# Layer 0's entry by chunks of four tokens, modulation work on GpSimd, k scaled by a power

## The reference

```python
mod = (_silu(L0_c) @ L0_wmod).reshape(L0_c.shape[0], 6, 1, -1)
sa, ca, ga, sb, cb, gb = (mod[:, 0], mod[:, 1], mod[:, 2], mod[:, 3], mod[:, 4], mod[:, 5])
ga = (2 * (ga >= 0) - 1) * jnp.maximum(jnp.abs(ga), 0.25)
gb = (2 * (gb >= 0) - 1) * jnp.maximum(jnp.abs(gb), 0.25)
h = _layernorm(x, axis=-1) * (1 + ca) + sa
x = x + ga * _L0_attn_ref(h, ...)
```

```python
q = jax.nn.silu(x @ Wq).reshape(b, n, h, hd)
k = jax.nn.silu(x @ Wk).reshape(b, n, h, hd)
k = k * jax.lax.rsqrt(jnp.sum(k * k, -1, keepdims=True) + 1e-12)
v = (x @ Wv).reshape(b, n, h, hd)
beta = 2.0 * jax.nn.sigmoid(x @ Wbet)
a = jax.nn.sigmoid(x @ Wf)
def step(S, inp):
    qt, kt, vt, at, bt = inp
    Sd = at[..., None, None] * S
    u = vt - jnp.einsum('bhk,bhkv->bhv', kt, Sd)
    Sn = Sd + bt[..., None, None] * kt[..., None] * u[:, :, None, :]
    o = jnp.einsum('bhk,bhkv->bhv', qt, Sn)
    return (Sn, o)
```

## Time and profile before

| | before |
|---|---|
| median of 3 runs | 2143.96 us (2143.17 to 2151.37) |
| time of the profiled execution | 2147.42 us |
| its span | 2145.6 us |
| mean granted TensorE clock | 0.908 |
| busy: PE, DVE, ACT, POOL | 1723.7, 1363.8, 1163.1, 267.3 us |
| first instruction of the scan (L370) | starts at 75.19 us |

### The profile page before, as it was taken

One profiled execution on the slowest core, in us unless ns is written; L12 is line 12 of the kernel. 1 busy time (PEld: TensorE's weight loads), 2 busy tenths in 40 slices (PEclk: granted clock), 3 DMA queues, 4 the chain that ended last, 5 costly groups with the idle time before them and its releaser, 6 DMA issues.

```text
span 2145.6 us, 27944 instructions
## 1 busy us (share of the span) xinstructions
PE 1723.7 (80%) x10324; PEld 786.0 (37%) x10324; DVE 1363.8 (64%) x2683; ACT 1163.1 (54%) x2116; POOL 267.3 (12%) x336
## 2 busy tenths in 40 slices
PE   3599237269999999999875994989899988489998
PEld 2599225012222222222223442444444444334443
DVE  3898775599999999999622335556656656322222
ACT  3465103028888888888862336556666655212222
POOL 1265003000000000000000002111111111111110
PEclk7899658559999999999996996999999999699999
DMA  1000000430000000000012420000000000122320
GB/s 40 1 1 1 0 0 8 93 47 2 2 2 2 2 2 2 2 2 2 17 26 41 84 63 1 4 12 16 15 15 15 15 0 1 30 43 47 59 51 29
DMA packets 76094, 42.58 MB, mean 20 GB/s; under 512 B 21920, under 2 KB 72224, under 8 KB 75840
## 3 DMA queue, kind: packets, MB, share of 16 engines
q1 hardware_dynamic: 74576, 37.90, 8.6%
q10 hardware_dynamic: 1392, 3.02, 0.7%
HBM read 37.55 MB, written 3.15 MB: 19 GB/s over the span
## 4 chain that ended last, share of the span: by engine, by line
PE 52%; DVE 30%; ACT 7%; DMA 4%; issue 4%; POOL 1%; SPq 0%; ACTq 0%; DVEq 0%; POOLq 0%
DVE MX L865 17%; PE PS L1347 6%; PE PS L920 5%; PE PS L1353 5%; PE PS L1779 4%; PE PS L1780 4%; PE PS L1789 4%; PE PS L942 3%; DMA SB<-scr_w 3%; PE PS L433 3%; PE PS L1298 3%; ACT tmpb L986 3%; PE PS L1317 2%; PE PS L1189 2%; DVE MS L534 2%
## 5 line engine op out<-in xcount | busy, mean ns | idle before, releaser
L986 ACT ACTIVATE tmpb<-PS 128x512 f32<-128x512 f32 x1024 | 554.0, 595 | 143.0 <-PE PS L942 126.5
L865 DVE TENSOR_REDUCE MX<-PS 128x2 f32<-128x1024 f32 x512 | 585.3, 1217 | 52.7 <-PE PS L847 48.9
L920 PE MATMUL PS<-tmpb,VS 128*32 128x256 f32 x4096 | 326.4, 393 | 14.0 <-ACT tmpb L986 6.6
L847 PE MATMUL PS<-KST,QST 56*128 56x512 bf16 x1024 | 206.6, 401 | 61.6 <-DMA KST<-scr_k 34.3
L942 PE MATMUL PS<-QST,KST 59*128 59x512 bf16 x1024 | 201.4, 390 | 21.2 <-ACT tmpb L986 17.0
L1814 DVE TENSOR_TENSOR HG<-HG,PS 128x512 f32<-128x512 f32 (+1 forms) x96 | 65.9, 686 | 199.3 <-PE PS L1780 199.3
L1804 ACT ACTIVATE HG<-PS 128x512 f32<-128x512 f32 (+1 forms) x96 | 57.2, 595 | 207.7 <-PE PS L1779 207.7
L920 PEld LDWEIGHTS PS<-tmpb,VS 128*32 128x32 f32 x4096 | 82.5, 108 | 179.0 <-issue 85.0
L942 PEld LDWEIGHTS PS<-QST,KST 59*128 59x128 bf16 x1024 | 49.2, 93 | 244.3 <-ACT tmpb L986 229.8
L1347 PE MATMUL PS<-X,WF 128*128 128x512 f32 x256 | 128.4, 636 | 4.2 <-ACT X L1492 4.2
L1508 ACT ACTIVATE HF<-PS,CL 128x512 f32<-128x512 f32 x128 | 87.9, 687 | 68.7 <-PE PS L1347 68.7
(11 more groups left out here) (293 smaller groups left out, 2491.5 us busy)
## 6 DMA issues: line engine op xcount, KB each, us to landing
SB<-scr_w SPq DMA_DIRECT2D x16, 1024.0 KB, 14.4
WF<-in_L_attn_Wf SPq DMA_DIRECT2D x16, 256.0 KB, 3.0
QST<-NMP SPq DMA_DIRECT2D x192, 1.0 KB
G<-in_L_ffn_w SPq DMA_DIRECT2D x16, 176.0 KB, 2.4
QST<-scr_q SPq DMA_DIRECT2D x14, 192.0 KB
W<-in_L_ffn_w SPq DMA_DIRECT2D x16, 128.0 KB, 2.1
scr_q<-tmpb SPq DMA_DIRECT2D x3, 512.0 KB, 2.7
KST<-scr_k ACTq DMA_DIRECT2D x14, 96.0 KB
```

Of the source, the lines that this page charges most:

```text
L847: pe.matmul(PS[:, b + x, :], QST[r, 2 * g + jj, CH * qc + P * t:CH * qc + P * t + P], KST[r, g, cs(kc)], start=True, stop=True).then_inc(s ...
L865: r = v.tensor_reduce(MX[:, :, m // (TPC * NC), m // NC % TPC, m % NC], PS[:, b:b + 2, :], AX.X, ALU.max)
L920: last = pe.matmul(PS[32 * j:32 * j + 32, 3, h], VS[:, kt, u // NC, :], PB[:, kt % 2, j, h], start=(kt == 0 and half == 0), stop=(kt == NT ...
L986: a.activation(PB[:, kt % 2, j, :], PS[:, at % 3, :], ACT.Exp, scale=HD ** -0.5).then_inc(s_exp, 1)
```

## The change

The layernorm of the first chunk now needs only two modulation columns. x arrives in four transfers with a semaphore each. The two columns sa and ca of layer 0 are multiplied first (L273) and copied by DVE between two chunks' statistics. Chunks 0 and 1 are normalised and transposed through two PSUM banks, and projecting, normalising and k's products alternate by chunk. Of the other modulation vectors only what later code reads is computed: four rows of layer 0 in one matmul of 512 columns, and eight columns. Adding 1, the gates and Wo's two factors are done on POOL (`g_mods`). The Silu is a Sigmoid and a product. Instead of a square root on ACT and a reciprocal on DVE, POOL raises the sums of squares to -0.5, chunk by chunk, 128x64 numbers each (`g_krs`, L350). k's unit form of the last chunk is made in the second step of the scan. `s_mod` is waited for after the scan.

```diff
         def sp_pre(sp):
-            sp.dma_start(X[:, :, :], A["L0_attn_x"][0].rearrange("(p s) d -> p s d", p=P)).then_inc(s_x, 16)
+            for c in range(NC):
+                sp.dma_start(X[:, ts_(c), :], A["L0_attn_x"][0].rearrange("(p s) d -> p s d", p=P)[:, ts_(c), :]).then_inc(s_xc[c], 16)
...
         def act_pre(a):
             for l in range(2):
-                a.dma_start(ccol[:, l:l + 1], A[f"L{l}_c"].rearrange("a d -> d a")).then_inc(s_mod_in, 16)
-                a.dma_start(wm[:, l, :], A[f"L{l}_wmod"]).then_inc(s_mod_in, 16)
-            a.wait_ge(s_mod_in, 64)
-            a.activation(scol[:, :], ccol[:, :], ACT.Silu).then_inc(s_sc, 1)
+                a.dma_start(ccol[:, l:l + 1], A[f"L{l}_c"].rearrange("a d -> d a")).then_inc(s_cc, 16)
+            for l in range(2):
+                a.dma_start(wm[:, l, :], A[f"L{l}_wmod"]).then_inc(s_wm[l], 16)
+            a.wait_ge(s_cc, 32)
+            a.activation(sgc[:, :], ccol[:, :], ACT.Sigmoid).then_inc(s_sg, 1)
...
+        def pe_mods(pe):
+            pe.wait_ge(s_wm[1], 16)
+            pe.wait_ge(s_mc, 1)
+            pe.matmul(ROW, scb[:, :], wm[:, 0, 2 * D:6 * D], start=True, stop=True)
+            for l, j in ((0, 3), (0, 4), (1, 0), (1, 1), (1, 2), (1, 3), (1, 4), (1, 5)):
+                last = pe_col(pe, l, j)
             last.then_inc(s_modps, 1)
...
+        def pe_a0(pe):
+            pe_first_cols(pe)
+            pe.wait_ge(s_const, 1)
+            pe_turn_x(pe, 0)
+            pe_turn_x(pe, 1)
+            pe_qkv(pe, 0)
+            pe_mods(pe)
+            pe_qkv(pe, 1)
+            pe_turn_x(pe, 2)
+            pe_qkv(pe, 2)
+            pe_turn_x(pe, 3)
+            pe_qkv(pe, 3)
...
+        def act_a0(a):
+            norm_apply(a, SM, X, 0, 0)
+            norm_apply(a, SM, X, 0, 1)
+            act_feat_x(a, 0)
+            act_feat_x(a, 1)
+            act_qkv(a, range(0, 4))
+            norm_apply(a, SM, X, 0, 2)
+            act_qkv(a, range(4, 6))
+            act_feat_x(a, 2)
+            act_qkv(a, range(6, 8))
+            norm_apply(a, SM, X, 0, 3)
+            act_qkv(a, range(8, 10))
+            act_feat_x(a, 3)
+            act_qkv(a, range(10, NT))
             act_state(a)
...
+        def g_krs(g, c):
+            g.wait_ge(s_kn2, c + 1)
+            k = kn2[:, TPC * H0 * c:TPC * H0 * (c + 1)].rearrange("p (s h) -> p s h", s=TPC)
+            g.tensor_tensor(k, k, mhalf[:, 0:1].unsqueeze(2).to_broadcast([P, TPC, H0]), ALU.pow).then_inc(s_krs, 1)
...
+        def g_mods(g, chain):
+            g.wait_ge(s_modv, 1)
+            for m in (modr[:, 0, 4, :], modc[:, 0, 4:5], modc[:, 1, 1:2], modc[:, 1, 4:5]):
+                last = g.tensor_scalar(m, m, 1.0, None, ALU.add)
+            chain.link(last)
+            g_gate(g, chain, modr[:, 0, 2::3, :], gt[:, 0, :, 0:D], gt[:, 1, :, 0:D])
+            g_gate(g, chain, modc[:, 1, 2::3], gt[:, 0, :, D], gt[:, 1, :, D])
+            g.wait_ge(s_w0, 7 * 16)
+            chain.link(g.tensor_scalar(Wo0[:, :], Wo0[:, :], nw0[:, 0:1], None, ALU.mult))
+            chain.link(g.tensor_tensor(Wo0[:, :], Wo0[:, :], modr[:, 0, 2, :], ALU.mult))
+            g.sem_inc(s_mod, 1)
...
+        def v_ksum(v, chain, c):
+            a = ts_(c)
+            v.wait_ge(s_aev, TPC * (c + 1))
+            k = QK[:, a, D:2 * D]
+            beta, alpha = SG[:, a, 2 * D:2 * D + H0], SG[:, a, 2 * D + H0:NQ]
+            chain.link(v.tensor_tensor(KN[:, a, :], k, k, ALU.mult))
+            chain.link(v.tensor_reduce(kn_(c), KN[:, a, :].rearrange("p s (h i) -> p (s h) i", i=HD), AX.X, ALU.add))
+            v.tensor_scalar(kn_(c), kn_(c), 1e-12, None, ALU.add).then_inc(s_kn2, 1)
             chain.link(v.tensor_scalar(beta, beta, 2.0, None, ALU.mult))
...
+            v.scalar_tensor_tensor(ba[:, a, :], alpha, -1.0, beta, ALU.mult, ALU.mult)
+            chain.link(v.tensor_tensor(four(V0[:, a, :]), four(V0[:, a, :]), over(beta), ALU.mult))
+
+        def v_kunit(v, chain, c):
+            a = ts_(c)
+            v.wait_ge(s_krs, c + 1)
...
+        def v_a0(v, chain):
+            v_qk(v, 0)
+            v_ksum(v, chain, 0)
+            v_qk(v, 1)
+            v_kunit(v, chain, 0)
+            v_modcopy(v)
+            v_ksum(v, chain, 1)
+            v_qk(v, 2)
+            v_kunit(v, chain, 1)
+            v_ksum(v, chain, 2)
+            v_qk(v, 3)
+            v_kunit(v, chain, 2)
+            v_ksum(v, chain, 3)
             v_ka(v, 0, 0)
             for s in range(NT):
+                if s == 1:
+                    v_kunit(v, chain, 3)
                 v_ka(v, s, 1)
...
             for c in range(NC):
                 norm_rstd(g, chain, SM, 0, c, False)
+            g_krs(g, 0)
+            g_mods(g, chain)
+            for c in range(1, NC):
+                g_krs(g, c)
             g_a0(g, chain)
```

More of the change, by code:

```diff
@@ L95, in build @@
         s_done = sem("s_done")
[L96 to L99, removed]
+        s_xc = [sem(f"s_xc{c}") for c in range(NC)]
+        s_cc, s_wm = sem("s_cc"), [sem(f"s_wm{l}") for l in range(2)]
+        s_sg, s_sc, s_mcp, s_mc = sem("s_sg"), sem("s_sc"), sem("s_mcp"), sem("s_mc")
+        s_modps, s_modv, s_mod = sem("s_modps"), sem("s_modv"), sem("s_mod")
         s_w0 = sem("s_w0")
@@ L191, in build @@
         ccol = sb("ccol", [P, 2], F32, a0)
-        scb = sb("scb", [P, 2, P], F32, a0)
+        sgc = sb("sgc", [P, 2], F32, a0)
+        scb = sb("scb", [P, P], F32, a0)
         gt = sb("gt", [P, 2, 2, D + 1], F32, a0)
@@ L223, in build @@
         s_amm, s_asig, s_av, s_aev = sem("s_amm"), sem("s_asig"), sem("s_av"), sem("s_aev")
-        s_kn2, s_ksq = sem("s_kn2"), sem("s_ksq")
+        s_kn2, s_krs = sem("s_kn2"), sem("s_krs")
         s_state, s_as, s_pr, s_w, s_kw = sem("s_state"), sem("s_as"), sem("s_pr"), sem("s_w"), sem("s_kw")
@@ L265, in g_pre @@
                             base=0, pattern=[[-1, P]], channel_multiplier=1).then_inc(s_const, 1)
[L267 to L276, removed]
-            last.then_inc(s_modps, 1)
@@ L279, in v_pre @@
[L279 to L306, removed]
@@ L309, in pe_a0, with pe_col, pe_first_cols @@
-        def pe_a0(pe):
+        ROW, COL = PS[:, 5, :], PS[:, 4, 0:12].rearrange("p (l j) -> p l j", l=2)
+        def pe_col(pe, l, j):
+            return pe.matmul(COL[:, l, j:j + 1], wm[:, l, j * D:(j + 1) * D], scol[:, l:l + 1], start=True, stop=True)
+        def pe_first_cols(pe):
+            pe.wait_ge(s_sc, 1)
+            pe.wait_ge(s_wm[0], 16)
+            pe_col(pe, 0, 0)
+            pe_col(pe, 0, 1).then_inc(s_mcp, 1)
+        def pe_mods(pe):
[4 more added lines that the diff above has]
+                last = pe_col(pe, l, j)
+            last.then_inc(s_modps, 1)
@@ L310, in pe_a0, with pe_turn_x, pe_qkv @@
+        def pe_turn_x(pe, c):
+            pe.wait_ge(SM["normed"], c + 1)
+            pe.sem_inc(SM["normg"], 1)
+            if c >= 2:
+                pe.wait_ge(SM["feat"], c - 1)
+            for j, t in enumerate(tiles(c)):
+                last = pe.transpose(PS[:, 6 + c % 2, P * j:P * j + P], XN[:, t, :], ident[:, :])
+            last.then_inc(SM["turned"], 1)
+        def pe_qkv(pe, c):
             pe.wait_ge(s_w0, 7 * 16)
-            for s in range(NT):
-                pe.wait_ge(SM["feat"], s // TPC + 1)
+            pe.wait_ge(SM["feat"], c + 1)
+            for s in tiles(c):
@@ L316, in pe_a0, with act_feat_x, act_qkv @@
                 pe.matmul(PS[:, s % 4, 0:NQ + D], HT[:, P * s:P * s + P], WC[:, :], start=True, stop=True).then_inc(s_amm, 1)
-        def act_a0(a):
-            for s in range(NT):
+        def pe_a0(pe):
[10 more added lines that the diff above has]
+            pe_qkv(pe, 3)
+        def act_feat_x(a, c):
+            a.wait_ge(SM["turned"], c + 1)
+            a.wait_ge(s_mc, 1)
+            a.activation(HT[:, cs(c)], PS[:, 6 + c % 2, :], ACT.Identity, scale=modc[:, 0, 1:2], bias=modc[:, 0, 0:1]).then_inc(SM["feat"], 1)
+        def act_qkv(a, tokens):
+            for s in tokens:
                 a.wait_ge(s_amm, s + 1)
@@ L322, in act_a0 @@
                 a.activation(V0[:, s, :], PS[:, s % 4, NQ:NQ + D], ACT.Copy).then_inc(s_av, 1)
-            a.wait_ge(s_kn2, 1)
-            a.activation(kn2[:, :], kn2[:, :], ACT.Sqrt).then_inc(s_ksq, 1)
-            act_state(a)
-        def v_a0(v, chain):
-            for s in range(NT):
+        def act_a0(a):
[12 more added lines that the diff above has]
+            act_qkv(a, range(10, NT))
+            act_state(a)
@@ new lines, in g_krs, with g_gate @@
+        def g_krs(g, c):
+            g.wait_ge(s_kn2, c + 1)
+            k = kn2[:, TPC * H0 * c:TPC * H0 * (c + 1)].rearrange("p (s h) -> p s h", s=TPC)
+            g.tensor_tensor(k, k, mhalf[:, 0:1].unsqueeze(2).to_broadcast([P, TPC, H0]), ALU.pow).then_inc(s_krs, 1)
+        def g_gate(g, chain, m, s, t):
+            chain.link(g.tensor_scalar(s, m, 0.0, 2.0, ALU.is_ge, ALU.mult))
+            chain.link(g.tensor_scalar(s, s, -1.0, None, ALU.add))
```

(50 more changed lines are left out.)

## The result

The changed kernel takes 2159.47 us (median of 12 runs, 2152.65 to 2163.89), the kernel before 2151.05 us over 12 runs (2140.57 to 2157.23). The ratio is 1.0043, with a 95% interval of 1.0024 to 1.0062: slower by 5 to 13 us, at the median by 8.4. That lies in the range, on the side that was forecast, and at about a third of the forecast's 24 us; by its time, 0.43%, it falls inside the prediction's bound of 0.5%, in the case between. The forecast of 2168 us was counted from a median of 2143.96 over three runs, and twelve runs gave 2151.05; part of the closeness of 2159 to 2168 comes from that, and the difference of 8.4 against 24 is the fairer comparison. Two single runs far outside all others (2693 us of the kernel before, 3205 us of one experiment) are not in the ratios.

The account below looks back on a forecast made before the run. The entry's chain of waits to the scan's start was taken as the bound: that start moves from 75.19 to 97.6 (+22.4), plus 1.45 for unit k, +23.9 us in all, giving 2168 us on the median 2143.96; range 2120 to 2177.

Parts of the forecast that it names:

- bound of 0.5%: Whole time: 10.7 us, about what a measurement can tell from no change; passed with a power over 10.3 or under 4.9.
- the case between: Rival on POOL: the power is partly pipelined, between 4.9 and 10.3 us, time within 0.5%; 2141 us at 7; chance 0.15.
- The mechanism: Entry up to the scan: powers, g_mods and clearing on POOL join the path; the scan's start moves by +22.4 us.
- 43.2 + 4p: Start of the scan in us, with p for the length of one power on POOL; even at p = 7.6.
- the signs that were named: Profile checks: scan start within 4 us of 43.2 + 4p, nothing behind L455 differing by over 2 us, among others.
- By column: POOL's power: its excess over a product is paid on each column, 13.6 us for 64 columns; slower, chance 0.52.
- last chunk's unit k: DVE, second step of the scan, which has hardly room: adds 1.45 us.
- paid once: Rival on POOL's power: the excess is a fixed part, 1.15 us a power; 2118 us; once or nearly, chance 0.33.
- The hold: DVE's two-input operations are held during a POOL power; without it the sum would be 5.2 us smaller.
- g_mods was too cheap: POOL, in front of chunk 1's power: 16 instructions and 12 waits of g_mods put at 6.4 us, to 44.5.
- The beginning: Entry up to the first sums: transfers, statistics, normalising and projection let the first power start at 19.45 us.
- The clearing: POOL, behind the last power: clearing SH and SA takes 3.45 us, now exposed before the scan's first instruction, to 97.6.

Follow-up runs that it names:

- The widths: The kernel before, with six more powers of 1, 2, 8, 16, 32 and 128 columns on POOL in idle time; the single execution took 2158.1 us.
- The clearing first: Against the changed kernel, POOL clears SH and SA before the first power instead of behind the last one; 2146.03 us, ratio 0.9981 to the kernel before.

## Why the prediction came out as it did

**The mechanism was right.** The four powers, `g_mods` and the clearing are the path, as the chain shows, and the sign hung on the length of one power. By the prediction's own formula, 43.2 + 4p, the measured 10.52 us give 85.3, and the scan started at 83.06. At the measured p the forecast would have been 85.3 + 1.45 - 75.19 = +11.5 us, against +8.8 at the mark behind the scan and +8.4 between the medians. Of the signs that were named, the start outside 43.2 + 4p by over 4 us did not come (it was 2.2 under), and up to the mark behind the scan the difference behind L455 was 0.9 us; beyond it, it was 4.9 in this one profile, over the 2 us that were allowed, and no edit explains it.

**The step that failed is the size of the power.** "By column: 0.21 a column, 64 x 0.21 + 0.2 = 13.6 us" took all of the excess over a product at 4 columns as slope. The widths give 0.16 a column on a fixed 0.40. That is 3.1 us a power and 12.3 in the sum, out of the 15.1 us between the forecast's +23.9 and the +8.8 at the mark. The other 2.8 are the 2.2 by which the start lay under the formula, and 0.6 on the last chunk's unit k. One width cannot tell a fixed part from a slope, and the end "paid once", at 1.15, was 9.4 us a power off; but an edit with four powers in line multiplies the error by four.

**The chances were set wrong for the same reason.** The case between was given 0.15, as "Nothing in the rows speaks for this but that both ends are extremes". By the length of a power, 10.52 us, the measurement lies just outside it, over its upper bound of 10.3, and its mechanism, a power that is partly pipelined, was not seen: the widths show a slope on every column. By the time, 0.43%, it lies inside, because the rest came out 2.8 us under the sum. So a fixed part of twice the product's was enough to bring the sum to the edge of that case, and a single width had left this open.

**The hold was wrong and cost nothing in the sign.** "During a power DVE's two-input operations are held" carried over from a product. No hold of over 0.3 us was seen, and none later than 0.5 us after the start of a power. This takes the 5.2 us out that the text named. The Trainium skill (SBUF — State Buffer, section "Who interferes with whom") calls the sharing an exclusive lock, and has a DVE instruction with two inputs from SBUF contend with a GpSimd instruction that reads SBUF. The rows agree for a product; for a power a lock of the instruction's whole length is not what they show, and the measurement decides.

**g_mods was too cheap.** 6.4 us were put down, and it took 8.9 (32.50 to 41.36). Its operations with one input at 256 columns take 0.85 and 0.88 us (L356, L354), and 1.11 where DVE's two-input L409 and L410 ran beside it (L353), where 0.5 with an upper end of 0.66 was taken; those with two inputs take 0.63 to 0.68, as predicted. This and the hold leave the start 2.7 us earlier together, near the 2.2 by which it lay under the formula.

**The beginning** was right to a tenth by luck, since its errors cancel: the first power began at 19.58 against 19.45. x's first chunk landed after 3.85 us instead of 3.0, but the condition vector came early enough to let the Sigmoid run at 5.62 instead of 7.5, so that POOL had chunk 1's scale at 9.53 instead of 11.0. ACT then waited 1.7 us (0.61, 0.81 and 0.25) for PE's projections in the first four tokens, which the sum had at ACT's pace of 0.70 each. ACT's first normalisation, at 7.81, was as predicted (about 8). The granted clock was 1.00 to 30 us, so TensorE's lower level cost nothing there.

**The last chunk's unit k** was put at 1.45; the scan to the mark took 0.9 longer (144.46 against 143.54). Its second half met a product on POOL (L416 at 95.90 took 2.39 us, and 0.69 elsewhere), and even so the whole price did not show; that its step had some waiting left would explain this, and was not tested.

**The clearing** cost its 3.5 us, and more than the prediction saw: it tied the scan to the last power, which the experiment "The clearing first" untied for 12.4 us.

## What to carry to other kernels

Before a short operation is used at another width, measure it at two widths: the fixed part and the slope decide what four of them in line cost, and one width gives neither. When work goes to a lightly used engine, look at which of its instructions now stand behind that work in its queue, and who waits for them; the clearing here moved the start of the scan by 12 us, and the products behind `g_mods` made DVE wait 12.5, without being long. Where an engine that bounds a loop waits in each step, single pieces of moved work that are as long as the wait go in nearly free: nine pieces of 0.55 to 0.7 us cost 1.8 us together, and in blocks 9.6.
